# Two attention blocks of a 4x16x16x128 image batch: every matrix stage rebuilt on 32-row, 32-column and 64x32 tiles of TensorE

## What is computed

```python
f = xf @ wf + bf;  g = xf @ wg + bg;  hv = xf @ wh + bh      # 16, 16 and 64 channels
beta = softmax(einsum('bnd,bmd->bnm', g, f))                 # first scores, 256 x 256 per image
o = einsum('bnm,bmd->bnd', beta, hv) @ wo + bo
y = relu(batch_norm(concat([gamma * o + xf, xf]) @ wc + bc))
qt = conv1x1(y, w_q, b_q).reshape(32, 256, 16)               # 4 images x 8 heads
xp = avg_pool_3x3_s2_same(y)                                 # 64 pooled pixels per image
kt, vt = (conv1x1(xp, w, b).reshape(32, 64, 16) for (w, b) in ((w_k, b_k), (w_v, b_v)))
attn = softmax(einsum('bnd,bmd->bnm', qt, kt) / 4)           # second scores, 256 x 64 per head
out = conv1x1(einsum('bnm,bmd->bnd', attn, vt).reshape(4, 16, 16, 128), w_o, b_o) + y
```

## Time and profile before

| | |
|---|---|
| timed runs | 56.82, 57.2, 58.84 us; median 57.2 |
| span of the profiled execution, first to last instruction | 55.1 us |
| busy PE / PEld / DVE / ACT / POOL | 50.0 / 39.5 / 39.4 / 30.3 / 13.6 us |
| chain that ended last | PE 84%, DVE 9%, ACT 1%, issue 1% |

### The profile page before, as it was taken

One profiled execution on the slowest core, in us unless ns is written; L12 is line 12 of the kernel. 1 busy time (PEld: TensorE's weight loads), 2 busy tenths in 40 slices (PEclk: granted clock), 3 DMA queues, 4 the chain that ended last, 5 costly groups with the idle time before them and its releaser, 6 DMA issues.

```text
span 55.1 us, 960 instructions
## 1 busy us (share of the span) xinstructions
PE 50.0 (91%) x320; PEld 39.5 (72%) x320; DVE 39.4 (71%) x114; ACT 30.3 (55%) x75; POOL 13.6 (25%) x25
## 2 busy tenths in 40 slices
PE   2999999999999999999999999999999998589620
PEld 2956678978875488999668999947899942559410
DVE  1005289429595499959889988989996889997930
ACT  4603076745689979998407998532975800443000
POOL 6999990000570000093000019100021000000000
PEclk9999999999999999999999999999999999999996
DMA  0799400000000000000000000000001100002311
GB/s 0 172 291 366 164 12 0 0 0 0 0 12 0 0 0 0 0 6 6 0 0 0 0 0 12 0 0 0 0 0 53 42 0 0 0 0 78 112 48 48
DMA packets 1300, 1.96 MB, mean 36 GB/s; under 512 B 144, under 2 KB 912, under 8 KB 1296
## 3 DMA queue, kind: packets, MB, share of 16 engines
q1 hardware_dynamic: 1296, 1.91, 10.7%
HBM read 1.38 MB, written 0.52 MB: 35 GB/s over the span
## 4 chain that ended last, share of the span: by engine, by line
PE 84%; DVE 9%; ACT 1%; issue 1%
PE bk_o L391 11%; PE bk_k L350 9%; PE bk_s1a L370 7%; PE bk_k L416 7%; PE bk_y L323 6%; PE bk_s1b L370 5%; PE bk_fg L266 4%; PE bk_s0a L300 4%; PE bk_s1b L376 4%; PE bk_fg L338 4%; PE bk_y L319 3%; PE bk_s0b L300 3%; DVE d L640 3%; PE bk_y L357 3%; PE bk_s0a L310 2%; PE bk_s1a L376 2%
## 5 line engine op out<-in xcount | busy, mean ns | idle before, releaser
L520 ACT ACTIVATE p<-d 128x512 f32<-128x512 f32 x8 | 5.0, 630 | 7.8 <-DVE d L640 7.7
L238 POOL TENSOR_TENSOR p0n<-p,rsum 128x256 f32<-128x256 f32 x6 | 3.5, 612 | 20.9 <-DVE rsum L596 20.9
L391 PE MATMUL bk_o<-v_heads,pt 128*128 128x34 f32 x56 | 6.9, 276 | 0.0
L391 PEld LDWEIGHTS bk_o<-v_heads,pt 128*128 128x128 f32 x56 | 6.6, 192 | 0.1
L350 PE MATMUL bk_k<-xp,late 128*80 128x64 f32 x64 | 5.3, 235 | 0.0
L515 ACT COPY k_heads<-k_rows 32x128 f32<-32x128 f32 x16 | 4.7, 296 | 0.7
L350 PEld LDWEIGHTS bk_k<-xp,late 128*80 128x80 f32 x64 | 4.9, 151 | 0.3 <-DVE xp L605 0.2
L416 PE MATMUL bk_k<-warm 128*128 128x128 f32 x14 | 3.8, 431 | 1.1 <-DVE warm L680 1.1
L623 DVE COPY k_heads<-k_rows 32x128 f32<-32x128 f32 x16 | 4.4, 277 | 0.3
L370 PE MATMUL bk_s1a<-k_heads,q_heads 128*128 128x512 f32 x8 | 4.3, 615 | 0.1
L416 PEld LDWEIGHTS bk_k<-warm 128*128 128x128 f32 x14 | 3.0, 307 | 1.8 <-DVE warm L680 1.1
(11 more groups left out here) (115 smaller groups left out, 107.5 us busy)
## 6 DMA issues: line engine op xcount, KB each, us to landing
late<-in_late SPq DMA_DIRECT2D x1, 522.5 KB, 5.7
x_rest<-in_x_rest SPq DMA_DIRECT2D x1, 384.0 KB, 4.8
out_t<-res SPq DMA_DIRECT2D x3, 128.0 KB, 1.8
prep<-in_prep SPq DMA_DIRECT2D x1, 291.5 KB, 2.9
first<-in_first SPq DMA_DIRECT2D x1, 153.5 KB, 2.2
out_t<-res SPq DMA_DIRECT2D x2, 64.0 KB, 1.6
```

The lines of the kernel that those rows point to most:

```text
L238: nc.gpsimd.tensor_tensor(p0n[:, b, t, :], p0[:, b, t, :], rsum0[:, b, t:t + 1].to_broadcast([P, N]), ALU.mult).then_inc(p0_pool, 1)
L391: last = mm(o_ps[b][s][:, k * 2 * VW:(k + 1) * 2 * VW], pt1[:, b, s, k, :], v_heads[:, b, s * 2 + k % 2].rearrange("m h v -> m (h v)"), st ...
L520: sc.activation(p1[:, b, s, :], d1[:, b, s].rearrange("n h m -> n (h m)"), ACT.Exp, scale=1.0 / TEMP).then_inc(exp1_done, 1)
```

## The change

All four inputs and the output stay the same; what changes is the shape of nearly every TensorE operation, and with it what the other engines do.

- f and g are computed four times, into four groups of 32 partitions (`project_fg`: eight matmuls of 32 weight columns, 128 moving columns). `scores_0` becomes four matmuls that each use 32 rows, into four banks.
- `queries` becomes 16 matmuls of 32 weight columns and 64 moving columns, which leave the queries already in the layout of the heads. `keys_values` becomes one matmul of 256 columns; VectorE then turns keys and values in blocks of 32 (`turn_k`, `turn_v`) and makes the two masked copies of the keys (`make_keys`). The block-diagonal buffer, its copies and `turn_q` are gone.
- `scores_1` is eight matmuls of 32 rows into four banks; VectorE takes all maxima of an image at once (`max_1`, 1024 columns). The maxima are turned by TensorE (`turn_max`), copied (`keep_max`), and the scores are computed a second time with keys and queries exchanged (`scores_t`), the negative maximum being added in the accumulation by a matmul with an indicator (`shift_t`). ScalarE's exponential then reads PSUM and writes what `attend_1` uses, so `turn_1`, its copies and VectorE's subtraction are gone.
- `attend_1` is 16 matmuls on tiles of 64 rows by 32 columns; VectorE turns the result (`turn_o`, 512 columns), normalises, TensorE turns it again, ScalarE copies it, and `conv_1` follows.
- x_rest is loaded in two transfers, the last result is stored in one; GpSimd takes some pooling, normalising and residual work. One table per stage says which bank and engine each image uses.

```diff
-                mm(fg_bank[b][0:48, 0:N], f_("wfg"), image(b), start=True, stop=True).then_inc(fg_ps, 1)
+                for k in range(4):
+                    mm(bk[Q * k:Q * k + Q, bf, 0:P], f_("wf"), image(b)[:, k % 2 * P:k % 2 * P + P], start=True, stop=True)
+                for k in range(4):
+                    last = mm(bk[Q * k:Q * k + Q, bg, g_at:g_at + P], f_("wg"), image(b)[:, k // 2 * P:k // 2 * P + P],
+                              start=True, stop=True)
...
-                mm(bk_s0[t][:, 0:N], g[:, b, t * P:(t + 1) * P], f[:, b, :], start=True, stop=True).then_inc(s0_ps, 1)
+                for k in range(4):
+                    r = slice(Q * k, Q * k + Q)
+                    last = mm(bk[:, S0_BANK[b] + k, 0:P], fg[r, b, 1, :], fg[r, b, 0, :], start=True, stop=True)
...
+                for i in range(I):
+                    for j in range(J):
+                        last = mm(out[Q * j:Q * j + Q, :, i], l_("wq")[:, Q * i:Q * i + Q], px, start=True, stop=True)
...
-                mm(bk_s1[s][:, :], q_heads[:, b, s].rearrange("c i p -> c (i p)"),
-                   k_heads[:, b, s].rearrange("c e j m -> c (e j m)"), start=True, stop=True).then_inc(s1_ps, 1)
-            def turn_1(b, s):
-                    last = turn(bk_s1[s][:, k * P:(k + 1) * P], p1[:, b, s, k * P:(k + 1) * P], ident)
+                for s in range(S2):
+                    for j in range(J):
+                        last = mm(bk[:, S1_BANK[b] + j, s * P:(s + 1) * P], q_(b, s, j), k_(b, s, j), start=True, stop=True)
+            def scores_t(b):
+                        mm(bk[:, ST_BANK[b] + j, s * P:(s + 1) * P], k_(b, s, j), q_(b, s, j), start=(s == 0), stop=False,
+                           skip_group_check=True)
+            def shift_t(b):
+                        last = mm(bk[:, ST_BANK[b] + j, s * P:(s + 1) * P], l_("ind", r)[:, s * P:(s + 1) * P], max_t[r, b, :],
+                                  start=False, stop=True, skip_group_check=True)
...
+                for j in range(J):
+                    for e in range(E):
+                        r = slice(M * e, M * e + M)
+                        last = mm(bk[Q * j:Q * j + Q, O_BANK[b] + e, s * P:(s + 1) * P], vals[r, b, s * J + j, :],
+                                  pt1[r, b, s, j, :], start=True, stop=True)
...
-                sc.activation(p1[:, b, s, :], d1[:, b, s].rearrange("n h m -> n (h m)"), ACT.Exp,
+                sc.activation(pt1[:, b, s], group(ST_BANK[b])[:, :, s * P:(s + 1) * P], ACT.Exp,
...
-                step(v.tensor_reduce(max1[:, b, s, :], sc1, AX.X, ALU.max))
-                v.tensor_tensor(d1[:, b, s], sc1, max1[:, b, s, :].unsqueeze(2).to_broadcast([P, E * J, M]),
+                v.tensor_reduce(nmax1[:, b, :, 0:S2 * E], group(S1_BANK[b])[:, :, 0:S2 * P].rearrange("n j (k m) -> n j k m", m=M),
+                                AX.X, ALU.max, negate=True).then_inc(max1_ready, 1)
```

More of the change, by code:

```diff
@@ L69, in columns, with nth @@
     return out, at
+def nth(on, b):
+    return sum(e == on[b] for e in on[:b + 1])
 def build(nc, first_d, x_d, prep_d, late_d, out_t):
@@ L86, in build, with f_ @@
         first, prep, late = sb("first", n_f), sb("prep", n_p), sb("late", n_l)
-        def f_(name, rows=slice(0, P)):
-            return first[rows, at_f[name]]
+        def f_(name):
+            return first[:, at_f[name]]
         def p_(name, rows=slice(0, P)):
@@ L241, in bias_q @@
[L241 to L253, removed]
+            gp.tensor_tensor(rstd[:], var_eps[:], neg_half[:], ALU.pow).then_inc(rstd_ready, 1)
@@ new lines, in turn_o @@
+            def turn_o(b):
+                pe.wait_ge(*at(o_normed, OM_ON, b))
+                rows = o_rows[:, b].rearrange("n (s i) e d -> n s (i e d)", s=S2)
+                for s in range(S2):
+                    last = turn(bk[:, OC_BANK[b], s * P:(s + 1) * P], rows[:, s], ident)
+                last.then_inc(oc_ps, 1)
+            def conv_1(b):
+                pe.wait_ge(*at(oc_kept, OC_ON, b))
+                mm(bk[:, RES_BANK[b], 0:N], l_("wo1"), o_cols[:, b, :], start=True, stop=True).then_inc(res_ps, 1)
@@ L420, in _ @@
             weights_1()
-            fill(1)
-            scores_0(0, 0)
-            scores_0(0, 1)
+            pe.wait_ge(f_act, 1)
+            pe.wait_ge(g_dve, 1)
+            scores_0(0)
+            project_fg(1)
             weights_2()
-            project_fg(1)
-            fill(1)
+            project_fg(2)
+            pe.wait_ge(wow_kept, 1)
+            project_fg(3)
+            pe.wait_ge(fg_dve, 1)
+            values_0(0)
+            pe.wait_ge(w3_kept, 1)
+            pe.wait_ge(c_kept, 1)
@@ L439, in _ @@
-            turn_values(0)
-            turn_0(1, 0)
-            turn_0(1, 1)
-            project_fg(3)
-            for b in range(B):
-                if b >= 1:
-                    turn_values(b)
-                if 1 <= b < LAST:
-                    turn_0(b + 1, 0)
-                    turn_0(b + 1, 1)
-                scores_1(b, 0)
-                scores_1(b, 1)
-                if b + 1 < B:
-                    conv_0(b + 1)
-                if b >= 2:
-                    conv_1(b - 2)
-                if b + 2 < B:
-                    scores_0(b + 2, 0)
-                    scores_0(b + 2, 1)
-                turn_1(b, 0)
-                if b + 1 < B:
-                    queries(b + 1)
-                if b == LAST:
-                    conv_1(LAST - 1)
-                turn_1(b, 1)
-                if b + 1 < B:
-                    keys_values(b + 1)
-                attend_1(b, 0)
-                attend_1(b, 1)
@@ new lines, in _ @@
+            queries(0)
+            pe.wait_ge(y_kept, 1)
+            conv_0(1)
+            pe.wait_ge(pt0_kept[0]["act"], 2)
+            turn_0(2, 0)
+            pe.wait_ge(exp0_done, 6)
+            scores_0(3)
+            pe.wait_ge(pt0_kept[1]["dve"], 2)
+            keys_values(0)
+            pe.wait_ge(q_copied, 1)
+            turn_0(2, 1)
+            pe.wait_ge(y_kept, 2)
+            queries(1)
+            pe.wait_ge(pt0_kept[0]["act"], 3)
+            conv_0(2)
+            pe.wait_ge(pt0_kept[1]["act"], 1)
@@ new lines, in _ @@
+            turn_values(0)
+            pe.wait_ge(v_turned, 1)
+            turn_0(3, 0)
+            pe.wait_ge(exp0_done, 8)
+            scores_1(0)
+            pe.wait_ge(q_copied, 2)
+            queries(2)
+            pe.wait_ge(vals_made, 1)
+            turn_0(3, 1)
+            pe.wait_ge(y_kept, 3)
+            keys_values(1)
+            pe.wait_ge(pt0_kept[0]["act"], 4)
+            keys_values(2)
+            pe.wait_ge(q_copied, 3)
+            conv_0(3)
+            pe.wait_ge(max1_ready, 1)
@@ new lines, in _ @@
+            scores_t(0)
+            pe.wait_ge(pt0_kept[1]["act"], 2)
+            turn_max(0)
+            pe.wait_ge(v_turned, 2)
+            turn_values(1)
+            pe.wait_ge(y_kept, 4)
+            queries(3)
+            shift_t(0)
+            pe.wait_ge(max_kept["act"], 1)
+            pe.wait_ge(q_copied, 4)
+            pe.wait_ge(v_turned, 3)
+            pe.wait_ge(vals_made, 2)
+            scores_1(1)
+            pe.wait_ge(exp1_done, 2)
+            scores_1(2)
+            pe.wait_ge(max1_ready, 2)
@@ new lines, in _ @@
+            turn_values(2)
+            turn_max(1)
+            keys_values(3)
+            pe.wait_ge(max1_ready, 3)
+            scores_t(1)
+            turn_max(2)
+            shift_t(1)
+            pe.wait_ge(vals_made, 3)
+            pe.wait_ge(max_kept["act"], 3)
+            attend_1(0, 0)
+            attend_1(0, 1)
+            turn_values(3)
+            pe.wait_ge(exp1_done, 4)
+            scores_1(3)
+            pe.wait_ge(o_turned, 1)
+            pe.wait_ge(vals_made, 4)
+            pe.wait_ge(v_turned, 4)
@@ new lines, in _ @@
+            scores_t(2)
+            shift_t(2)
+            pe.wait_ge(max1_ready, 4)
+            attend_1(1, 0)
+            turn_max(3)
+            attend_1(1, 1)
+            turn_o(0)
+            pe.wait_ge(exp1_done, 6)
+            scores_t(3)
+            pe.wait_ge(max_kept["dve"], 1)
+            pe.wait_ge(oc_kept["act"], 1)
+            attend_1(2, 0)
+            shift_t(3)
+            attend_1(2, 1)
+            pe.wait_ge(o_turned, 2)
+            attend_1(3, 0)
+            pe.wait_ge(exp1_done, 8)
@@ L471, in _ @@
+            turn_o(1)
+            attend_1(3, 1)
+            turn_o(2)
+            conv_1(0)
+            pe.wait_ge(o_turned, 3)
+            conv_1(1)
+            conv_1(2)
+            pe.wait_ge(oc_kept["act"], 2)
+            turn_o(3)
+            conv_1(3)
         @block.scalar
```

909 lines of the change are left out of this document (480 added, 429 removed).

## The result

The changed kernel takes 47.43, 47.44 and 47.58 us, the kernel before 56.82 and 57.2 in the same comparison: a ratio of 0.834, 95% interval 0.829 to 0.839, so about 17% faster. The forecast was 50.0, inside a range of 44 to 62.5. The execution that was profiled took 47.58 us and its span is 45.7. Some executions of most kernels here (one of the changed kernel at 51.32 us, two of the kernel before at 58.8) are about 2 to 5 us longer than the others of the same kernel: times and ratios leave them out, but the profiles of e1, e2 and e6 were taken in such longer ones.

The account below looks back on a forecast made before the run. TensorE was taken as the bound: 40.9 us of work from 3.6 on, plus 0.7 waiting, less 4.6 ordered later, gives 40.6; the tail leads to 45.8, 2.1 to a 47.9 span, another 2.1 to 50.0 us, range 44 to 62.5.

Parts of the forecast that it names:

- What bounds the kernel: Whole kernel: TensorE, 84% of the chain before, stays the bound at 40.9 us; VectorE about 30, ScalarE about 22.
- The pace of tiled passes, 0.033 us: All tiled groups: passes with small tiles start every 0.033 us, giving 4.5 us of tiled work per image.
- the first rival: Tiled TensorE groups: tiles run fully side by side, 0.028 us a pass, 45 us in all; chance 0.18.
- The change of shape, 0.13: TensorE: each change of tile shape costs 0.13 us; 44 changes cost 5.7 us.
- The exposed wait, 0.7 us: scores_1 of image 2 waits for both exponentials of image 0; 0.7 us exposed, later ones covered by attention.
- two more waits: Second attention, if tiles run fully side by side: two waits for a second maximum, 1.24 each partly covered, about 1.5 us.
- 40.9 less 4.6: TensorE's sum from 3.57 us on, less work ordered after the last image's shift_t, which then ends at 40.6 us.
- The tail, 5.2 us: Last image after shift_t: exponentials, half attention, VectorE's turn and normalising, conv_1, addition, from 40.6 to 45.8 us.
- The second: Tiled groups: passes start in program order, so a matmul's second pass holds up the next tile; 62 us, chance 0.22.
- Queued weight loads: scores_0, scores_1, scores_t, shift_t: weight loads of row groups queue, 0.077 us more a pass; 67 us, chance 0.09.
- no overlap: Tiled groups: tiles don't run beside each other at all, 13.3 us of tiled work per image; 85 us, chance 0.06.
- The granted clock: TensorE: if the clock falls to half in the waits, passes cost double in those stretches and the sum is wrong.

Follow-up runs that it names:

- e1: Changed kernel with the loops over tiles and repetitions exchanged in five groups, so neighbouring matmuls use the same tile: 50.9 us, ratio 0.896.
- e2: Changed kernel with first scores, second scores, transposed scores and shift all reading the same first 32 rows (one row tile): 79.95 us.
- e6: Changed kernel with f, g and the first scores on wide matmuls as in the kernel before: 51.6 us, ratio 0.906.
- e7: Changed kernel with unread matmul groups behind its last result: 32 passes on four row tiles took 1.10 us in turn, 2.75 with four matmuls in a row per tile.
- e10: Changed kernel with unread groups behind its last result, unbroken or alternating in tile shape: alternating groups took 3.16, 3.41 and 3.10 us.
- e5: Changed kernel with second-softmax probabilities turned by TensorE, as in the kernel before, instead of scores computed twice: 56.6 and 57.1 us, ratio 0.999.
- e3: Changed kernel without the second softmax's maximum: scores_1, the reduction, its turn, copy and shift left out: 44.1 us, ratio 0.776.

## Why the prediction was right, and where its numbers were not

**What bounds the kernel: right.** TensorE was the path, VectorE with 28.0 us and ScalarE with 20.6 stayed below it as forecast (30 and 22). The side and the range hold.

**The pace of tiled passes, 0.033 us: too slow.** This step failed: the line through `keys_values` and `attend_1` gave a pace of starts that no group with its tiles in turn shows. Measured is what the first rival said, which had a chance of 0.18: 0.11/4 = 0.028 for 128 columns, 0.056/4 = 0.014 for `queries` (0.58 less 0.14 for the change, in eight rounds), 0.014 for the eight tiles of `attend_1`. Per image 2.9 us of tiled work instead of 4.5, 6.5 less in all (e7 and e10 measured it by itself, for four tiles and 128 columns). For four row tiles the Trainium skill (TensorE: Matmul & The Clock Gate, Part 3) gives 3.07 times, with 512 columns. The 3.0 of e2 (1.98 against 0.66) is near it, but has a change of shape in each group; without the change, 0.2 in both, it is 3.9.

**The change of shape, 0.13: too cheap.** e10 gives 0.14 to 0.21, which on 44 changes is 6.2 to 9.2 us instead of 5.7, so 0.5 to 3.5 more. By kind, 12 into row tiles, 16 into the full array, 7 into column tiles, 6 into the 64x32 tiles (0.16) and 3 others, it is about 8, some 2.5 more. The two errors partly cancel, and that is luck.

**The exposed wait, 0.7 us: too little.** The forecast named the wait of `scores_1` for exponentials; it is there twice, probably since `attend_1` shrank and no longer covers the second. The maxima come on top, as the first rival had it ("two more waits"). Together 1.6 us by the waits view ahead of the last `shift_t`.

The windows of the changed kernel up to that `shift_t` give the balance (TensorE busy 22.62 + 9.75 = 32.4 us):

```profile
3.50:26.20 22.70, 22.62 (x352) 17.49 (x355) 16.15 (x44) 11.79 (x37) 8.59 (x18) 1.00 0.13 42
26.20:37.70 11.50, 9.75 (x243) 6.86 (x250) 7.94 (x16) 4.16 (x9) 1.46 (x3) 1.00 0.02 4
```

The forecast had 36.3 us of work (40.9 less 4.6) and 0.7 of waiting, to 40.6. Measured are 32.4 and 1.8, to 37.69: 3.9 less work, 1.1 more waiting, 2.9 earlier.

**The tail, 5.2 us: measured 5.8.** The forecast followed VectorE's turning and normalising. The chain goes through TensorE instead: `conv_1` of the three other images (1.30) stands in the order ahead of the last turn. The store and what lies around the span came out 0.1 later and 0.2 shorter. With -2.9, +0.6, +0.1 and -0.2 the 50.0 becomes 47.6, the profiled run.

**The rivals.** The first had the mechanism, and its 45 lacked the full price of the changes and some of the waits. The second (program order, 62 us) is not what happens with tiles in turn, where the first passes on the other tiles start before a matmul's second pass. The Trainium skill (same part) has matmuls start strictly in program order. By these starts that does not hold for the second passes. The rival comes near where four matmuls in a row share a tile: 2.75 us in e7. Queued weight loads and no overlap are excluded by 0.66 for 16 passes. The granted clock, named as what would make the forecast wrong, stayed full here and fell in e2, e5, e6 and e7.

**The second computation of the scores** is part of what makes the change pay. Turned probabilities on the same tiles stand where the kernel before stood (e5); of the 9 to 9.5 us that this loses, up to 6.2 are the clock's, and the 3 that are left hold for the changed kernel's order alone. The maximum, with the scores, turns and shift that serve it, costs 3.4 us (e3). Without it the softmax is the same in exact arithmetic, and these scores, from -8.2 to 6.9, don't need it; other data might.

## What to carry to other kernels

Deal tiled matmuls out over the tiles in turn, and count two prices: a pass divided by the tiles that run side by side, and some 0.14 to 0.21 us for each change of shape, so that a group of eight passes pays as much for its change as for its work. The length of a wait on the chain is not what its removal gives: see what the engine does meanwhile, since that work moves onto the chain. Count the time that TensorE saves only as far as its waits don't take it back.

## What the runs showed of the hardware that was not expected

- The second passes of matmuls are overtaken by first passes on other tiles (6 to 7 ns apart), but TensorE looks only a little way ahead: with four matmuls in a row on each tile, 32 passes cost 2.75 us instead of 1.10.
- Passes on different tiles reach the full four times, and eight tiles the full eight (0.38 us for 16 passes, 0.16 of it for the change).
- The granted clock fell to half while TensorE's row showed nines, after passes that used one row tile (e2 from 35 us on, e7 at 53.1), and after stretches with waits (e5). In e6 it fell some 1.2 us after a `scores_0` on one row tile (1.10 us), and then stood at half to 18 us, though TensorE was busy throughout and more than half of that time on the full array. What it takes for the clock to fall or rise was not tried apart. In the changed kernel, with TensorE's row between 4 and 9 in the middle, it didn't fall before the end.
